# Linear attention and a two-expert feed-forward on one core: new orders in five stretches, and 19 extra products

## The reference, cut to what matters

```python
# attention layer, 16 heads of 8
q, k, v = silu(x @ Wq), silu(x @ Wk), x @ Wv
q, k = [t*cos(ang), t*sin(ang)], ...          # ang = theta * position
energy = (q @ k.T) * tril                     # no softmax
out = (energy @ v) @ Wo * sigmoid(x @ G1 @ G2)
out = normed(out) * gamma + beta
x = normed(x + out)
# feed-forward: a shared part for all tokens, and 2 of 8 experts for each token
probs = softmax(rms_normed(x) @ router_w.T); the two best per token
dispatch = the first 1280 tokens of each expert, in token order
routed[dispatch] += weight * ((silu(xg @ rg) * (xg @ ru)) @ rd)
shared = silu(x @ sg) * (x @ su) @ sd
x = normed(x + shared + routed)
```

## Time and profile before

| | us |
|---|---|
| runs | 858.65, 861.96, 870.18 |
| profiled execution, its own time | 858.42 |
| its span, first to last instruction | 856.6 |
| PE busy | 808.4 (94%) |
| DVE busy | 611.7 (71%) |
| POOL busy | 400.2 (47%) |
| ACT busy | 355.7 (42%) |

### The profile page before, as it was taken

How to read it: one execution, slowest core, us unless ns; L and a number is a source line. 1 busy time by engine, 2 the same in 40 slices (tenths; PEclk the granted TensorE clock), 3 DMA queues, 4 the chain that set the end, 5 groups by cost and what they waited for, 6 DMA issues and landing times.

```text
span 856.6 us, 27882 instructions
## 1 busy us (share of the span) xinstructions
PE 808.4 (94%) x11178; PEld 658.8 (77%) x11178; DVE 611.7 (71%) x1941; ACT 355.7 (42%) x744; POOL 400.2 (47%) x375
## 2 busy tenths in 40 slices
PE   5989999999999999999999898889999999999995
PEld 3667787777777777777777676668999999998875
DVE  6576978979797897979788988864445444443675
ACT  6333544535445453535443332223333333222575
POOL 7522141333224133323415545464487787777433
PEclk9899999999999999999999999999999999999998
DMA  5135111111121111112122221032345555433454
GB/s 146 30 108 209 39 51 44 43 45 42 37 52 49 42 44 45 43 39 52 39 60 54 66 48 46 3 107 81 79 96 96 97 100 97 65 51 31 124 159 136
DMA packets 74095, 59.89 MB, mean 70 GB/s; under 512 B 10163, under 2 KB 63722, under 8 KB 73968
## 3 DMA queue, kind: packets, MB, share of 16 engines
q1 hardware_dynamic: 56944, 41.84, 17.5%
q0 software_dynamic: 17024, 16.28, 10.5%
HBM read 23.99 MB, written 28.89 MB: 62 GB/s over the span
## 4 chain that ended last, share of the span: by engine, by line
PE 78%; DVE 12%; issue 4%; POOL 2%; DMA 1%; ACT 1%; DVEq 0%; POOLq 0%; ACTq 0%; SPq 0%
PE bank L1671 6%; PE bank L1673 5%; PE bank L1672 5%; PE energy_banks L1730 5%; PE energy_and_gate_banks L1671 5%; PE bank L1775 4%; PE bank L2190 4%; PE energy_and_gate_banks L1755 4%; PE energy_and_gate_banks L2190 4%; PE energy_and_gate_banks L1673 3%; PE energy_and_gate_banks L1672 3%; PE energy_banks L1671 3%; PE energy_banks L1673 3%; PE energy_banks L1672 3%; PE energy_banks L1723 2%
## 5 line engine op out<-in xcount | busy, mean ns | idle before, releaser
L559 POOL DMA_INDIRECT dispatched_rows<-x,slot x128 | 131.2, 1025 | 199.8 <-PE energy_banks L1730 113.6
L671 POOL DMA_INDIRECT summed_rows<-VP,goal_i x80 | 124.4, 1555 | 42.0 <-issue 22.5
L1001 ACT ACTIVATE sq<-energy_banks 128x512 f32<-128x512 f32 (+1 forms) x96 | 50.6, 527 | 120.0 <-PE energy_banks L1673 118.3
L1143 DVE TENSOR_TENSOR sf<-sf,bank 128x512 f32<-128x512 f32 x88 | 60.4, 686 | 38.0 <-PE bank L1673 36.7
L629 POOL TENSOR_TENSOR rr<-vq,minus_half 128x8 f32<-128x8 f32 x16 | 26.7, 1668 | 103.5 <-DVE vq L1213 103.5
L743 ACT ACTIVATE hidden_rounded<-sf 128x512 fp32r<-128x512 f32 x88 | 55.5, 631 | 39.2 <-DVE sf L1143 39.2
L733 ACT ACTIVATE sf<-energy_and_gate_banks 128x512 f32<-128x512 f32 x88 | 52.7, 599 | 35.3 <-PE energy_and_gate_banks L1673 32.4
L1115 DVE TENSOR_TENSOR EM<-energy_and_gate_banks,causal 128x512 f32<-128x512 f32 x64 | 44.0, 688 | 26.8 <-PE energy_banks L1755 20.8
L706 ACT ACTIVATE sq<-bank 128x512 f32<-128x512 f32 x64 | 38.3, 599 | 48.4 <-PE bank L1673 46.0
L1775 PEld LDWEIGHTS bank<-VP,Kt 64*64 64x64 f32 x896 | 35.5, 134 | 29.3 <-issue 17.9
L1730 PE MATMUL energy_banks<-EM,VP 64*32 64x64 f32 x4096 | 56.6, 229 | 0.0
(11 more groups left out here) (239 smaller groups left out, 2264.2 us busy)
## 6 DMA issues: line engine op xcount, KB each, us to landing
QM<-QT SPq DMA_DIRECT2D x248, 32.0 KB
dispatched_rows<-empty POOLq DMA_DIRECT2D x8, 655.0 KB
QM<-dispatched_rows SPq DMA_DIRECT2D x8, 655.0 KB, 5.8
xin<-in_x SPq DMA_DIRECT2D x16, 256.0 KB, 2.8
QM<-summed_rows SPq DMA_DIRECT2D x16, 256.0 KB, 2.8
out_x<-QM SPq DMA_DIRECT2D x16, 256.0 KB, 3.2
summed_rows<-empty SPq DMA_DIRECT2D x13, 256.0 KB, 2.0
dispatched_rows<-x,slot POOLq DMA_INDIRECT x128
```

Of the source, the lines that this page charges most:

```text
L559: g.indirect_dma_start(out=xg_d, out_offset=bass.IndirectOffsetOnAxis(ap=slot[:, n % 2, j:j + 1], axis=0), in_=x1[:, n % 2, j % NC, :], in ...
L671: g.indirect_dma_start(out=sum_d, out_offset=bass.IndirectOffsetOnAxis(ap=goal_i[:, par, t:t + 1], axis=0), in_=ye[:, par, t, :], in_offse ...
L1143: v.tensor_tensor(sf[:, n % SF], sf[:, n % SF], UB[:], ALU.mult).then_inc(v_h, 1)
```

## The change

Seven things. (1) In the opening POOL's two table products go to DVE, `input_turned(1)`, `input_hi(1)` and `input_lo(1)` move from step 0 to step -1 and use bank `UB`, ACT takes the fourth `silu` ahead of the values, and PE issues 8, 2, 2, 3 and 4 products of 128x128 by 128x512 whose result nobody reads (`keep_busy`, bank `GB`). (2) In step 1 `centre` goes ahead of the third mask. (3) In steps 12 to 14 `shared_hidden` of the second pair goes ahead (of `add_input` in step 12, of the second moments in 13 and 14), and `slots` goes into the next step, behind `input_lo`; `positions` no longer waits for the masked state where its bank isn't the state's. (4) In step 15 the choices go ahead of the centring, `positions` ahead of the last attention chunk but one, `slots` ahead of the second moments. (5) In the passage all engines have new orders: above all `shared_add(SPARE)` on DVE now stands behind all eight `spread_hidden(RELOADED, f)` and `scale_x1(B, 1)`, and the routing of step 17 on PE stands behind the down products. (6) The semaphore `g_sc` is split into a fill count and two for even and odd blocks, and a dispatch waits for the fill alone. (7) POOL issues the first dispatch of block step 15 ahead of the power of that step. SP's list is the same but for the names of the semaphores.

```diff
+        def dispatches(n):
+            return P * (n // 2) if n > 1 else 0
+        def input_bank(n):
+            return (UB if n == 1 else PB[0])[:]
...
 # SP, b == B + 1
-                    sp.wait_ge(g_sc, P * (B + 1))
+                    for n in (B, B + 1):
+                        sp.wait_ge(g_sc[n % 2], dispatches(n))
 # POOL
-            gp.wait_ge(c_sin, 1)
-            for i in (0, 1):
-                g.tensor_tensor(products[:, i], coarse[1][:, i], fine[0][:, i], ALU.mult).then_inc(g_prod, 1)
...
-                    need(gp, g_sc, P * (n - 1))
+                    need(gp, g_fill, P)
...
-                        if n == B - 1 and j == 3:
+                        if n == B - 1 and j == 4:
                             first_rstd(B)
...
+                if b == B - 1:
+                    dispatch(b, (0,))
 # ACT, opening
-                    for i in (0, 1, 2):
+                    for i in range(4):
                         silu(f, fp, i)
                     act.wait_ge(z_vp, 1)
                     values(f, fp, 0)
-                    silu(f, fp, 3)
                     values(f, fp, 1)
+                    input_hi(1)
                     keys_by_token()
 # DVE, opening
+            def table_product(i):
+                link(v.tensor_tensor(by_place[:, i], coarse[0][:, i], fine[1][:, i], ALU.mult))
             def table_sum(i):
-                need(dve, g_prod, i + 1)
+                link(v.tensor_tensor(products[:, i], coarse[1][:, i], fine[0][:, i], ALU.mult))
                 link(v.tensor_tensor(table[:, i], table[:, i], KT[:, 0, i], ALU.add))
...
-                    for i in (0, 1):
-                        link(v.tensor_tensor(by_place[:, i], coarse[0][:, i], fine[1][:, i], ALU.mult))
+                    table_product(0)
                     table_sum(0)
+                    table_product(1)
                     turn(f, fp, 0)
                     table_sum(1)
                     turn(f, fp, 1)
                     turn(f, fp, 2)
                     turn(f, fp, 3)
+                    input_lo(1)
 # DVE, first_blocks
                     if back:
                         gate_moments(b)
+                        centre(b)
                     mask(b, par, 2)
...
                     if back:
-                        centre(b)
                         add_input(b)
 # DVE, steps 13 and 14
                     else:
                         input_lo()
+                        slots(b - 1, 1 - par)
                         mask(b, par, 0)
...
                         mask_state(b, 6)
-                        second_moments(b)
-                        mean_square(b)
                         shared_hidden(b, s1, SPARE)
                         mask(b, par, 3)
                         read_positions(b)
-                    slots(b, par)
+                        second_moments(b)
+                        mean_square(b)
 # DVE, step 15
+                    slots(b - 1, 1 - par)
                     mask(b, par, 0)
...
                     gate_moments(b)
+                    copy_logits(b)
                     hidden_lo(b, s0, SPARE)
-                    copy_logits(b)
                     mask_state(b, 4)
+                    two_best(b)
+                    choices(b, par)
+                    mask(b, par, 2)
+                    mask_state(b, 5)
                     centre(b)
                     add_input(b)
...
                     mask_state(b, 6)
+                    read_positions(b)
                     mask(b, par, 3)
+                    slots(b, par)
                     second_moments(b)
-                    mean_square(b)
-                    read_positions(b)
-                    slots(b, par)
 # DVE, passage
+            rows_lo(RELOADED)
+            mean_square(B - 1)
+            gate_norm(B)
+            spread_hidden(RELOADED, 0)
+            gate_moments(B)
             scale_x1(B - 1, 0)
-            rows_lo(RELOADED)
-            gate_norm(B)
-            gate_moments(B)
-            spread_hidden(RELOADED, 0)
+            spread_hidden(RELOADED, 1)
+            centre(B)
+            spread_hidden(RELOADED, 2)
             copy_logits(B)
             two_best(B)
+            add_input(B)
+            spread_hidden(RELOADED, 3)
             choices(B, 0)
-            spread_hidden(RELOADED, 1)
-            centre(B)
-            add_input(B)
+            spread_hidden(RELOADED, 4)
             second_moments(B)
+            spread_hidden(RELOADED, 5)
             mean_square(B)
+            read_positions(B)
+            spread_hidden(RELOADED, 6)
+            slots(B, 0)
+            spread_hidden(RELOADED, 7)
+            scale_x1(B, 1)
             dve.wait_ge(m_x1[0], 16)
             shared_add(SPARE, x1t[:, 0], PB[0])
...
 # PE
+            def keep_busy(n):
+                for _ in range(n):
+                    t.matmul(GB[:], wqk_hi[:, 0:P], wqk_hi, start=True, stop=True)
...
                     pe.wait_ge(a_wq, 1)
+                    keep_busy(8)
                     pe.wait_ge(v_wq, 1)
                     for i in range(4):
                         project(f, i)
+                    keep_busy(2)
                     values_projected(0)
+                    keep_busy(2)
                     values_projected(1)
+                    input_turned(1)
+                    keep_busy(3)
                     keys_turned()
+                    keep_busy(4)
 # PE, passage, from project_out(B)
+            for f in range(3):
+                spread_pair(RELOADED, f)
             turn_x1(B, 0)
-            spread_pair(RELOADED, 0)
+            spread_pair(RELOADED, 3)
             logits(B)
-            spread_pair(RELOADED, 1)
+            spread_pair(RELOADED, 4)
+            spread_pair(RELOADED, 5)
             positions(B)
             down_back(SPARE, PB[0])
-            for f in range(2, 6):
-                spread_pair(RELOADED, f)
-            turn_x1(B + 1, 1)
             spread_pair(RELOADED, 6)
             spread_pair(RELOADED, 7)
+            turn_again(1, x1[:, 0])
+            spread_down(RELOADED, (0, 1))
+            turn_x1(B + 1, 1)
+            spread_down(RELOADED, (2,))
             logits(B + 1)
-            spread_down(RELOADED, (0, 1))
+            spread_down(RELOADED, (3,))
+            spread_pair(AGAIN, 0)
             positions(B + 1)
-            turn_again(1, x1[:, 0])
-            spread_down(RELOADED, (2, 3))
-            for f in range(8):
+            for f in range(1, 8):
                 spread_pair(AGAIN, f)
```

More of the change, by code:

```diff
@@ L2061, in positions @@
                 need(pe, v_M, 6 * (b - 2) + 3)
-                need(pe, v_S, NS * (last(b) + 1))
                 if no_ffn(b):
@@ L2065, in positions @@
                     need(pe, v_lg, b - 1)
+                else:
+                    need(pe, v_S, NS * (last(b) + 1))
                 o = position_bank(b)
```

87 lines of the change are left out of this document (41 added, 46 removed).

## The result

Twelve executions of the changed kernel gave a median of 865.63 us (858.42 to 869.8), and twelve of the kernel before 861.7 (858.65 to 870.67). The ratio is 1.0054, with a 95% interval of 1.0031 to 1.0077: the changed kernel is half a per cent slower. The profiled execution took 858.42 us, to the hundredth the time of the one before. So the two profiles alone would say "no change", and there are two questions: what moved inside the 858.4, and what the other executions lose.

What follows compares the result with a forecast made beforehand. PE was taken as the bound, busy 808.4 of 856.6 us. From 858.4: less 3.4 (opening, step 0), 2.5 (step 1), 5.4 (steps 13, 14), plus 11.7 (passage) gave 858.8; forecast 860, range 848 to 868.

Steps and rivals of the forecast that it cites:

- a sign of being wrong: Changes up to step 15: the forecast counts as wrong if they bring less than 7 us.
- Passage: Behind step 15: PE stands still 10 us for weights at the first down product; lost 11.7 us, bounds 7 and 15.
- The weights are no wait: Rival, passage: down columns could start at 562.9 without waiting for weights, 846.7 us in all; chance 0.17.
- Opening, steps 0 and 1: Start of the kernel: 3.4 us gained in opening and step 0, 2.5 in step 1, clock gains included.
- Steps 13 and 14: PE's waits for `shared_hidden` and the half clock behind them go; gained 5.4 us, bounds 2.0 and 6.6.
- half of the 3.5 us: Whole kernel: added to the sum because the median lies 3.5 us above the profiled time, giving 860.
- the three clock gains: Less half clock in opening and step 0 (1.9 us), step 1 (1.4) and steps 13 and 14 (1.5 each).
- the passage's clock loss: Passage: low clock after 10 us without work, a loss of 1.7 to 3.4 us, taken as 2.5.
- Slower by the clock: Rival, opening, passage and step 14: the clock takes over 2 us more than summed, 866.3 us; chance 0.18, lock included.
- the lock: Opening turns: DVE operations blocked beside POOL, up to 1.8 us each for two turns, 862.4 us; within the 0.18 chance.
- four places: Opening products at 0.43 (+3.4 us), the pause (+0.9), the wait for rows (+1.7), half clock of step 14 (+1.5).
- Fill without effect: Rival, opening: unread products do not help, the clock still falls near 22 us, 860.7 us; chance 0.15.

Runs made afterwards that it cites:

- turning SP's list: Changed kernel with the load of `sd_s` and of expert 0's weights ahead of `keep_sum(SPARE)` in SP's list: 0.9973, 874.95 us.
- 0.9963: Kernel before with the new orders of the opening, step 0 and step 1 alone, 19 unread products included: ratio 0.9963, 871.15 us.
- 0.9943: Kernel before with new opening and step 1, old orders behind, and unread products ahead of `positions` in steps 12 to 14: ratio 0.9943, 869.54 us.

## Why the prediction was wrong, and what in it was right

I forecast 860 us, a little below the 861.96 of before; the kernel came out above it, at 865.63. The parts of the loss, by the ratios of the runs: up to step 15 the changes gain 2.5 us (forecast 11.3), the passage costs 7.1 (11.7), together 4.6 lost (0.4), which the ratio of the first set gives too. I had also named a sign of being wrong, that the part up to step 15 brings less than 7 us. The first profile shows 11.7 there; the runs, with 2.5, meet the sign.

**Passage: right in cause, and in size in the profile.** Forecast: PE stands still 10 us at the first down product, 11.7 us lost in all. Profile: 9.7, and 11.8 lost. In repeated runs it costs less: 7.1 us (changed kernel against the one with the old passage), at the lower of my bounds, and 9.2 by itself (0.0105 of 876.45). The clock fell to half about 3 us into the wait; of the 10.2 us at half only the last 3 are work, and behind PE's wait for the rows come 3.4 more. That is the 3.4 to 6.8 from which I had taken 2.5 us of loss. "The weights are no wait" is refuted by the wait itself and by turning SP's list.

**Opening, steps 0 and 1: right in the profile, too large in the runs.** Forecast 5.9, first two profiles 7.5, runs 3.2 (0.7 to 5.8). The last turn of the opening ended at 16.66 (17.1 forecast), because DVE's ten operations met only one slow product beside POOL:

```profile
9.88 1.13 DVE L1105 TENSOR_TENSOR KT<-SM 128x512 f32<-128x512 f32 x1
...
32.36 2.69 DVE L1120 TENSOR_TENSOR KT<-sq,table 128x512 f32<-128x512 f32 x2
...
58.11 0.45 PE L1743 MATMUL energy_banks<-QT,SM 128*64 128x64 f32 x8 [1.28 <-DVE EM L1128]
```

The lock of DVE and POOL did strike the turns of step 0 (2.69 for two, beside POOL's subtraction), for 0.7 us of wait. The wait for the mask in step 1 fell from 1.84 to 1.28, not to 0.7.

**Steps 13 and 14: the step that failed.** "Both waits go, and with each the half clock behind it ... Gained 5.4; bounds 2.0 (the half clock stays) and 6.6." The waits at `positions` went. The first profile shows 4.4 us gained (and a clock of 1.00 throughout); the part by itself loses 3.0 and 3.9 us, and in the changed kernel it gains nothing (2.5 us up to step 15, 3.2 of them from the opening and step 1). I had named what is late next (the moments and `slots`, ahead of the first mask of the next step) and priced it as 1.1 us of wait in step 14 and 0.1 in step 15, with no clock, and the first mask of step 13 as nothing. In fact PE waits 1.5 to 1.67 us there in step 13 and 0.9 to 1.4 in step 14, and in three later profiles a stretch of half clock of 10.2 us starts at the wait of step 13. The later moments of step 15 also add 1.4 us at `turn_x1` where the old passage follows. The bounds were the error in form: the worst case was "the half clock stays" (which by my own terms leaves 2.4, not 2.0), while a wait that moves can bring more of it than the old one did. Part of the new wait is a second lock that I did not price. The last instruction of `slots` is now issued while POOL works on the next block's input. DVE and POOL in the changed kernel's first profile:

```profile
462.64 1.22 DVE L1280 TENSOR_SCALAR slot<-slotf 128x8 int32<-128x8 f32 x1
```

```profile
462.55 1.27 POOL L642 TENSOR_TENSOR xb<-xin,bet 128x512 f32<-128x512 f32 x1
```

It took 1.22 us, from 462.64 to 463.86, and POOL's operation, which had begun first, ended at 463.82. In the old kernel no such instruction took more than 0.24: 1.05 us more ahead of the mask that PE waits for, in step 13 and again in step 14 (1.21 at 487.89). The Trainium skill, "SBUF — State Buffer", who interferes with whom, says that a DVE `tensor_scalar` can enter the modes that take the port pair shared with GpSimd, and that the one which starts second is blocked until the first has ended; the trace agrees. What this lock is worth alone is open: with `slots` behind `mask_state(b, 1)` the instruction took 0.17 us each time, but the time went elsewhere (1.0043).

**The numbers.** The sum was 858.8 against the profile, which came out at 858.42. To it I added "half of the 3.5 us" between profile and median. That is the second error: the profile of before had 6.8 us of half clock before 50 us and 17 in all up to 550; my changes were costed on exactly those stretches, as if they stood there in every execution. The Trainium skill, "TensorE: Matmul & The Clock Gate", part 1, says that the moment at which the clock rises differs from run to run. I had cited it for the opening alone and kept the clock as a term; taken seriously in steps 13 and 14, where 3.0 of my 5.4 us were clock, it would have left 2.4 there. The runs agree with it: kernels with the same opening show between 0 and 10 us at half from 50 to 90 us. Without the three clock gains (1.9, 1.4 and 3.0) my sum is 865.1, and without the passage's clock loss as well 862.6, both ahead of the 1.7 us that I added; the runs gave 865.63. That the first agrees so well is partly luck, since the passage was cheaper and steps 12 to 15 dearer than in it.

**Slower by the clock**, a rival, stood at 866.3 with a chance of 0.18 (shared with the lock), and 865.63 is near it. That is luck in part too. Of its four places, the products on the path did not run at 0.43 us (they ran at 0.24); the pause cost about what I had; the wait for the rows came (3.8 us, and 3.4 at half clock behind it); and the half clock of steps 13 and 14 stayed, in the later profiles. It named the clock rightly and did not see that the waits would move.

**Fill without effect**, a rival: in the opening the products raise the clock early and cost 0.7 us, with no net gain shown; in waits of 1 to 2 us in steps 12 to 16 they leave less half clock each time. In the kernels with the old order there are 17 us of it from 445 to 550 us unfilled and some 6 filled (the profiles of 0.9963 and 0.9943).

**Left open.** Why the later sets' profiles are 4 to 6 us longer between steps 2 and 12 (358.4 us from the third chunk of step 2 to the first of step 12 in the first two profiles, 362 to 365 with one of 367 in the others) and 7 to 14 longer in steps 12 to 15, whatever the order; and why in those steps PE has waits of 0.4 to 1.2 us that no engine or DMA ends, which the first two profiles lack there:

```profile
PE energy_banks L1750 <- issue: 2.5, 6, 0.5
PE bank L2110 <- issue: 1.0, 1, 1.0
```

(waits of PE, 440 to 570 us, the changed kernel's second profile). The 6.8 us at half clock from 460 to 470 us stand behind the one of 1.0 us, at 459.36, and not behind a wait of the new order. VectorE has waits of 1.8 to 4.3 us for something "remote" in most of those profiles and in neither of the first two. These may be why steps 12 to 14 fall more often there. The eleven unprofiled executions of the first set had 0.975 to 0.983, so they lost clock as well, but no trace says where.

## What to carry to other kernels

A wait that is moved still costs, and what it costs in TensorE's clock is not what the old one cost. Follow it to its new place, and take a second profile before believing the first: one profiled execution, here the fastest of twelve, showed none of the 20 us at half clock in steps 12 to 14 that another had. Cost the clock as a spread over executions, not as a term read off one trace; the granted clock of every execution stands beside its time and can be averaged. Where waits of 1 to 2 us could not be removed, a few unread products in them, into a bank that was free, went with a higher mean clock in each of the four kernels that had them, and with the old orders gave the lowest ratio here. And an unneeded dependence in the queue that loads weights (a store and its landing ahead of a load) costs its full length as soon as TensorE gets there earlier.

## What the hardware showed that I had not expected

A wait of 1.65 us was followed by 10.2 us at half clock in one place and waits of 1.81 by 3.4 in another, in the same kind of step; a wait of 1.67 us in the first profile of the changed kernel was followed by none (the clock is 1.00 from 445 to 550 us):

```profile
465.30 0.45 PE L1800 MATMUL bank<-VP,Kt 64*64 64x64 f32 x8 [1.67 <-DVE SM L1137]
470.54 0.45 PE L1800 MATMUL bank<-VP,Kt 64*64 64x64 f32 x8 [0.82 <-DVE SM L1137]
```

So the length of a wait alone does not say whether the clock falls. And an operation of eight numbers per partition took seven times its usual 0.17 us because of a neighbour on another engine.
